# A fifth buffer for gathered expert rows in a mixture-of-experts kernel

## The chip, the cores and the metric

The kernel runs on one core of a Trainium2 chip. A core has TensorE (PE, matmuls; its weight loads are shown apart as PEld), VectorE (DVE), ScalarE (ACT), GpSimd (POOL) and SyncE (SP), each with its own instruction stream, joined by counting semaphores, and 16 DMA engines that carry transfers issued from SP's and POOL's queues. The metric is the device time of one execution in microseconds (us).

## The reference

The input is 4 sequences of 1024 tokens by 512 channels. Two residual blocks are computed: a time-mix attention with a linear recurrence, and a feed-forward block of a shared part and 64 routed experts.

```
x = x + layernorm(attention(layernorm(x)))
h = layernorm(x)
idx, w = router(h)              # 64 experts, 8 groups, best 4 groups, best 6 experts per token
                                # scores = sigmoid(h @ gate_w.T); the choice uses scores + e_bias
shared = relu(h @ su.T)**2 @ sd.T            # 512 -> 1024 -> 512
for each expert e:                           # at most 128 tokens each
    rows   = h[tokens of e]                  # 128 x 512
    y      = relu(rows @ w1[e].T)**2 @ w2[e].T   # 512 -> 256 -> 512
    routed[tokens of e] += gate * y
x = x + layernorm(shared + routed)
```

## The kernel before, in words

The 4096 tokens are worked on as 8 tiles of 512. After the attention and the routing, a long stretch interleaves two jobs in an order written out by hand: the shared part of tiles 3 to 7 (each 8 steps of an up and a down matmul group), and the 64 experts, two to a step from step 2 of tile 3 on (`experts_in`), ending with two steps of tile 7 done; the remaining steps of tile 7 hold no expert. At the end the sums are loaded back, normalised and added to the residual.

The layout of memory: `h` in HBM holds each token's normalised row of 512 and, behind it, its 64 gates (576 numbers in all, 288 KB for 128 tokens). `ysh` holds the shared part's result, to which the experts add.

One expert e goes through these steps:

- **Index.** DVE copies column e of the token list into one of four columns of `gather_token` (`index_gather`, L1643). For e of 4 and above it first waits until PE has turned expert e-4.
- **Gather.** POOL issues an indirect DMA of 128 rows of `h` into `xd_sb[e % 4]` (`gather`, L1196), after the index and after the turning of expert e-4. Three of the four buffers lie in the tile that the profile calls xres, one in xnd.
- **Turn.** PE transposes the rows in four pieces (`xd_transpose`, L668; here it waits for the rows), ACT copies them out (L1021).
- **First layer.** 16 small matmuls with w1 (`e_first`, L679), ACT takes relu and square (L1027, L1029), DVE squares and takes the rest of the rounding (`e_square`, L1657 and L1659).
- **Second layer.** w2 is split by ACT (`w2_round`, L1037) and DVE (`w2_rest`, L1663), then six matmuls (`e_second`, L694 to L696).
- **Gate.** ACT scales the result by the gate into one of four `e_out` buffers (`e_gate`, L1045, tile k_sb).
- **Scatter.** POOL issues an indirect DMA that adds the 128 rows into `ysh` (L1222). It waits for the gate step of e and for the landing of scatter e-1, since two experts may add to the same token.

The order on each engine at expert e matters. PE: turn e+2, first layer e+1, second layer e. ACT: copy of e+2, relu and square of e+1, gate e, split of w2 for e+1. DVE: square of e+1, then `index_scatter(e+1)` (L1650, L1652: the scatter's token column and the gate column, four of each; it waits for the landing of scatter e-3 and for the turning of e+1), then `index_gather(e+5)`, then `w2_rest(e+1)`. POOL: gather e+5, then scatter e. Before expert 0, POOL issues gathers 0 to 3, and at expert 0 gathers 4 and 5 before scatter 0. SP loads w1 and w2 (512 KB each, L369, four buffers each) as PE frees them, and a tile of `ht` (1 MB, L362) per tile of the shared part.

Small constants of the routing lie in the tile mixf as one row of 1024 numbers per partition (`consts`): the bias row in 0 to 63, expert numbers, masks, place numbers, and in 488 to 499 the three groups of four index and gate columns. Most of them have no reader once the token list is made.

Of the kernel before, what the change touches and what calls it, by code (L numbers as in the profile page):

```python
# [8 lines left out]
U32 = mybir.dt.uint32  # L9
# [5 lines left out]
C = 512  # L15
# [3 lines left out]
TT = 512  # L19
# [9 lines left out]
SJ = SH // P  # L29
IK = HID // P  # L30
ROUTE_SCALE = 2.5
EB, WB = 4, 4
LOWEST = 3e38
ROUTED = 3
RS = 3
# [11 lines left out]
def sandwich(nc, t):  # L47

    ctx = ExitStack()
    with ctx:  # L50
# [76 lines left out]
        yout_ready ysh_stored logits_done score_ready sel_ready pos_ready placed route_step gates_ready gates_stored hots_ready tabled table_ready  # L127
        gather_index scatter_index xd_turned xdT_ready e_up e_relu e_hi_ready e_square e_lo_ready w2_hi_ready w2_lo_ready e_down e_gated added
        out_stored o_summed ln4_stats ln4_moments ln4_based ln4_rstd o_joined o_normed o_ready o_added""".split()
        names += [f"{n}{q}" for n, b in (("w1_loaded", WB), ("w2_loaded", WB), ("xd_loaded", EB)) for q in range(b)]  # L130
        names += [f"{n}{k}" for n in ("ysh_loaded", "x1_loaded") for k in range(NT)]
        S = {n: sem(n) for n in names}

# [6 lines left out]
        def flat(tile):  # L140
            return tile[:, :, :].rearrange("p a b -> p (a b)")
# [14 lines left out]
        youts = [v_sb] * (ROUTED + 1) + [hb, sr, xin]  # L156
        consts = flat(mixf)
        bias_row = consts[:, 0:E]
        number = consts[:, E:2 * E]
        causal = consts[:, 128:192].bitcast(BF16)  # L160
        ones = consts[:, 192:256].bitcast(BF16)
# [6 lines left out]
        place_64 = consts[:, 640:640 + CAP]  # L168
        number_1 = consts[:, 768:768 + E]
        blank_row = consts[:, 832:833]  # L170
        gather_token = consts[:, 488:488 + EB].bitcast(U32)
        scatter_token = consts[:, 492:492 + EB].bitcast(U32)
        e_gates = consts[:, 496:496 + EB]
        scratch = flat(xnd)
        at = [0]

# [39 lines left out]
                 [state_flat[:, b * CK * HID:(b + 1) * CK * HID] for b in range(2)]  # L216
        w1_sb = [w.rearrange("p (k i) -> p k i", k=CK) for w in halves[0::2]]
        w2_sb = [w.rearrange("p (k c) -> p k c", k=IK) for w in halves[1::2]]
        xd_sb = [flat(xres)[:, q * (C + E):(q + 1) * (C + E)] for q in range(EB - 1)] + [scratch[:, 0:C + E]]
        xdT = [flat(xnT)[:, q * C:(q + 1) * C].rearrange("p (k n) -> p k n", k=CK) for q in range(EB)]  # L220
        e_hidden = [flat_run_max[:, b * HID:(b + 1) * HID] for b in range(2)]
        e_hi = [e_split[:, (2 + b) * HID:(3 + b) * HID] for b in range(2)]
# [69 lines left out]
        def within(e, ahead):  # L292
            return not (isinstance(e, int) and e + ahead >= E)
# [190 lines left out]
        def _(pe):  # L484
# [175 lines left out]


            def xd_transpose(e):
                q = e % EB
                pe.wait_ge(S[f"xd_loaded{q}"], 16 * (e // EB + 1))
                if e > 0:
                    pe.wait_ge(S["xdT_ready"], e)
                for c in range(CK):
                    mm = pe.transpose(turn_bank[:, c * P:(c + 1) * P], xd_sb[q][:, c * P:(c + 1) * P], ident[:, :])  # L668
                mm.then_inc(S["xd_turned"], 1)
# [449 lines left out]
        def _(pool):  # L1119
# [68 lines left out]
            scale_and_offset(3, NT - 1)  # L1188

            def gather(e):  # L1190
                q = e % EB
                pool.wait_ge(S["gather_index"], e + 1)
                if e >= EB:
                    pool.wait_ge(S["xd_turned"], e - EB + 1)
                pool.sem_inc(S["pool_step"], 1)
                pool.indirect_dma_start(xd_sb[q], None, t["h"], bass.IndirectOffsetOnAxis(ap=gather_token[:, q:q + 1], axis=0)).then_inc(S[f"xd_loaded{q}"], 16)  # L1196

# [2 lines left out]
            pool.wait_ge(S["h_blank"], 16)  # L1200
            pool.wait_ge(S["gates_stored"], 16 * NT)
            pool.wait_ge(S["h_lo_ready"], CK * (ROUTED + 1))
            for e in range(EB):
                gather(e)


# [1 line left out]
            def expert(e):  # L1208
                q = e % EB
                if first(e):  # L1210
                    gather(EB)
                if within(e, EB + 1):
                    gather(e + EB + 1)
                pool.wait_ge(S["e_gated"], e + 1)
                pool.wait_ge(S["scatter_index"], 2 * e + 2)
                if first(e):
                    pool.wait_ge(S["ysh_stored"], 16 * ROUTED)
                    pool.wait_ge(S["ysh_blank"], 16 * (1 + NT - ROUTED))
                else:
                    pool.wait_ge(S["added"], 16 * e)  # L1220
                pool.sem_inc(S["pool_step"], 1)
                pool.indirect_dma_start(t["ysh"], bass.IndirectOffsetOnAxis(ap=scatter_token[:, q:q + 1], axis=0), e_out[q], None,  # L1222
                                        compute_op=ALU.add).then_inc(S["added"], 16)
# [38 lines left out]
        def _(dve):  # L1262
# [373 lines left out]
                dve.tensor_tensor(s_lo[:, j % 3, :], square[:, j % 2, :], s_hi[:, j % 3, :].bitcast(F32), ALU.subtract).then_inc(S["s_lo_ready"], 1)  # L1636

            def index_gather(e):
                q = e % EB
                if e >= EB:  # L1640
                    dve.wait_ge(S["xd_turned"], e - EB + 1)
                    dve.sem_inc(S["dve_step"], 1)
                dve.tensor_copy(gather_token[:, q:q + 1], token_list[:, e:e + 1]).then_inc(S["gather_index"], 1)  # L1643

            def index_scatter(e):
                q = e % EB
                if e >= EB:
                    dve.wait_ge(S["added"], 16 * (e - EB + 1))
                    dve.sem_inc(S["dve_step"], 1)
                dve.tensor_copy(scatter_token[:, q:q + 1], token_list[:, e:e + 1]).then_inc(S["scatter_index"], 1)  # L1650
                dve.wait_ge(S["xd_turned"], e + 1)
                dve.tensor_copy(e_gates[:, q:q + 1], xd_sb[q][:, C + e:C + e + 1]).then_inc(S["scatter_index"], 1)  # L1652

            def e_square(e):
                b = e % 2
# [9 lines left out]
            def expert(e):  # L1665
                if e == 0:
                    index_scatter(0)
                    e_square(0)
                    w2_rest(0)
                if within(e, 1):  # L1670
                    e_square(e + 1)
                    index_scatter(e + 1)
                if e == 0:
                    index_gather(EB)
                if within(e, EB + 1):
                    index_gather(e + EB + 1)
                if within(e, 1):
                    w2_rest(e + 1)

            def tile(k):  # L1680
# [6 lines left out]
                for j in range(SJ):  # L1687
# [4 lines left out]
                    if k < ROUTED:  # L1692
                        if i == 1:
                            counted(r - 1, route_bank)
                        next_rest(*range(CK))
                        if i == 0 and r >= 2:
                            group_experts(r - 1)
                            experts_chosen(r - 1)
                        if i == 1:
                            hots(r - 1)  # L1700
                        if i == 2 and r < NT:
                            groups(r)
                        if n == 2:
                            ln3(NT - 1)
                    else:
                        todo = list(experts_in(k, j))
                        if k == ROUTED and j == 0:
                            list_tokens()
                            for e in range(EB):
                                index_gather(e)  # L1710
                        next_rest(0)
                        for e in todo[:1]:
                            expert(e)
                        next_rest(1)
                        for e in todo[1:2]:
                            expert(e)
                        next_rest(2)
                        for e in todo[2:]:
                            expert(e)
                        next_rest(3)  # L1720
# [74 lines left out]
```

## Time and profile before

| | us |
|---|---|
| median of 3 runs | 1281.77 |
| lowest and highest | 1281.32, 1287.52 |
| the profiled execution, its own time | 1278.08 |
| its span, first to last instruction | 1276.1 |
| busy: PE, DVE, ACT, POOL | 1151.0, 872.0, 682.9, 295.4 |

How to read it: the span is what the profile's positions are counted in, and the execution's time is 2.0 us more. Busy times are sums over an engine's instructions. A DMA's issue on POOL is counted as a POOL instruction; the transfer itself runs on after it, and "landing" is when its last part has arrived. A row names a line of the kernel and the tiles written and read, without buffer numbers.

### The profile page before, as it was taken

Reading aid. Unit: us, or ns where it says so; the run is one execution under the profiler, and the core shown is the slowest. Engines: PE = TensorE matmul, PEld = TensorE weight load, DVE = VectorE, ACT = ScalarE, POOL = GpSimd, SP = SyncE. Lnnn points to the kernel's source line nnn. Section 1 sums busy time; section 2 is a strip of 40 time slices with the busy share of each in tenths; the row PEclk is TensorE's granted clock in tenths of the full one; section 3 lists DMA queues with packets and bytes.
Section 4 is the critical chain, followed back from the end, with each engine's and each line's share of the span. In section 5 each row is a group of like instructions: output and inputs, shape, how many; then the busy total and the mean of one; then the engine's idle time right before and its main releaser. Section 6 shows DMA issues by size and latency. Waiting matters only on the chain.

```text
span 1276.1 us, 15911 instructions
## 1 busy us (share of the span) xinstructions
PE 1151.0 (90%) x5080; PEld 784.8 (61%) x5080; DVE 872.0 (68%) x2093; ACT 682.9 (54%) x1121; POOL 295.4 (23%) x268
## 2 busy tenths in 40 slices
PE   5997999899899997779999889999998999999893
PEld 2443444444344443457888768888887788788761
DVE  4598979897988898759888964444444344444384
ACT  2455656665667566763324235565555456555343
POOL 2010102020202001210000013443343443344255
PEclk9998999999999998789999999999999999999997
DMA  8401022222122241496534238989888888998798
GB/s 307 171 6 34 0 67 69 66 73 82 47 70 68 54 99 69 132 279 222 168 109 137 71 99 230 250 221 289 240 228 253 227 245 221 279 249 201 177 316 339
DMA packets 79520, 206.19 MB, mean 162 GB/s; under 512 B 10192, under 2 KB 10320, under 8 KB 76624
## 3 DMA queue, kind: packets, MB, share of 16 engines
q1 hardware_dynamic: 59408, 156.98, 35.3%
q0 software_dynamic: 20032, 48.24, 20.0%
q8 instruction: 38, 0.62, 0.2%
q14 instruction: 42, 0.34, 0.1%
HBM read 145.93 MB, written 59.28 MB: 161 GB/s over the span
## 4 chain that ended last, share of the span: by engine, by line
PE 26%; DMA 18%; DVE 6%; issue 3%; ACT 2%; POOL 2%; SPq 1%; POOLq 0%; DVEq 0%; ACTq 0%
DMA ysh<-k_sb,mixf 13%; PE bank L679 4%; PE bank L654 2%; PE bank L636 2%; PE bank L655 2%; PE bank L656 2%; PE bank L638 2%; PE bank L637 2%; DMA xnd<-h,mixf 2%; DMA xnd<-ysh 2%; PE bank L498 1%; DMA xres<-h,mixf 1%; PE bank L668 1%; PE bank L694 1%; PE bank L695 1%
## 5 line engine op out<-in xcount | busy, mean ns | idle before, releaser
L541 PE MATMUL bank<-mix_ring,weights 128*128 128x512 f32 x768 | 343.5, 605 | 14.2 <-ACT xres L848 7.0
L541 PEld LDWEIGHTS bank<-mix_ring,weights 128*128 128x128 f32 x768 | 147.2, 194 | 199.6 <-issue 193.2
L1222 POOL DMA_INDIRECT ysh<-k_sb,mixf x64 | 109.0, 1703 | 235.2 <-DVE mixf L1643 79.6
L548 PE MATMUL bank<-weights,rw 128*128 128x512 f32 x256 | 118.5, 618 | 12.5 <-ACT sr L807 9.0
L993 ACT ACTIVATE k_sb<-bank 128x512 f32<-128x512 f32 x64 | 38.2, 597 | 146.3 <-PE bank L638 146.2
L636 PE MATMUL bank<-h_high,ffn_w 128*128 128x512 f32 x256 | 102.9, 402 | 2.7 <-ACT k_sb L993 2.7
L1657 DVE TENSOR_TENSOR run_max<-run_max 128x256 f32<-128x256 f32 x64 | 27.2, 425 | 114.2 <-ACT e_split L1029 114.2
L654 PE MATMUL bank<-ffn_w,s_split 128*128 128x512 f32 x256 | 102.2, 399 | 0.3 <-DVE s_split L1636 0.3
L637 PE MATMUL bank<-h_low,ffn_w 128*128 128x512 f32 x256 | 100.9, 394 | 0.0
L638 PE MATMUL bank<-h_high,ffn_w 128*128 128x512 f32 x256 | 100.8, 394 | 0.0
L655 PE MATMUL bank<-ffn_w,s_split 128*128 128x512 f32 x256 | 100.7, 393 | 0.0
L656 PE MATMUL bank<-ffn_w,s_split 128*128 128x512 f32 x256 | 100.3, 392 | 0.0
L1196 POOL DMA_INDIRECT xres<-h,mixf x48 | 53.0, 1103 | 200.0 <-DVE mixf L1643 182.8
L548 PEld LDWEIGHTS bank<-weights,rw 128*128 128x128 f32 x256 | 50.4, 199 | 78.2 <-issue 66.1
L1133 POOL TENSOR_SCALAR rstd<-mv 128x4 f32<-128x4 f32 x16 | 9.9, 619 | 377.7 <-DVE mv L1285 369.7
L679 PE MATMUL bank<-xnT,wkv 128*128 128x128 f32 x768 | 93.7, 275 | 0.1
L1633 DVE TENSOR_TENSOR k_sb<-k_sb 128x512 f32<-128x512 f32 x64 | 44.1, 689 | 72.6 <-ACT k_sb L993 72.1
L1663 DVE TENSOR_TENSOR wkv_split<-wkv,xnd_split 128x1024 fp32r<-128x1024 f32 x48 | 58.8, 1224 | 47.4 <-ACT xnd_split L1037 45.9
L679 PEld LDWEIGHTS bank<-xnT,wkv 128*128 128x128 f32 x768 | 89.5, 192 | 0.3 <-issue 0.3
L1314 DVE SCALAR_TENSOR_TENSOR mix_ring<-xnd,vecs,xnT 128x512 f32<-128x512 f32 x96 | 70.1, 745 | 4.2 <-PE bank L541 2.1
L1045 ACT ACTIVATE k_sb<-bank,mixf 128x512 f32<-128x512 f32 x64 | 44.1, 689 | 48.1 <-PE bank L696 43.1
L694 PE MATMUL bank<-xnd_split,e_split 128*128 128x512 f32 x128 | 55.9, 436 | 10.5 <-ACT e_split L1029 6.7
(227 smaller groups left out, 2302.1 us busy)
## 6 DMA issues: line engine op xcount, KB each, us to landing
wkv<-in_w SPq DMA_DIRECT2D x96, 512.0 KB
state<-in_w SPq DMA_DIRECT2D x32, 512.0 KB
xin<-in_x SPq DMA_DIRECT2D x8, 1024.0 KB, 5.4
xin<-h SPq DMA_DIRECT2D x8, 1024.0 KB, 6.4
xres<-in_x POOLq DMA_DIRECT2D x7, 1024.0 KB, 9.2
h<-hb SPq DMA_DIRECT2D x7, 1024.0 KB, 4.5
x<-xres SPq DMA_DIRECT2D x7, 1024.0 KB, 6.8
ht<-xnT SPq DMA_DIRECT2D x7, 1024.0 KB, 8.2
```

What stands on the lines that cost most here:

```text
L541: mm = pe.matmul(bank[:, d, :], W(j)[:, ck, d * P:(d + 1) * P], mix_slot(4 * j + ck), start=(ck == 0), stop=(ck == CK - 1))
L548: mm = pe.matmul(bank[:, s, :], rw[:, ck, s * P:(s + 1) * P], W(3)[:, ck, :], start=(ck == 0), stop=(ck == CK - 1))
L636: pe.matmul(up_bank, hi, hT_hi[:, ck, :], start=(ck == 0), stop=False)
L637: pe.matmul(up_bank, hi, hT_lo[:, ck, :], start=False, stop=False)
L638: mm = pe.matmul(up_bank, lo, hT_hi[:, ck, :], start=False, stop=(ck == CK - 1))
L654: pe.matmul(y_bank[:, s, :], hi, w_hi, start=(j == 0), stop=False)
L655: pe.matmul(y_bank[:, s, :], hi, w_lo, start=False, stop=False)
L656: mm = pe.matmul(y_bank[:, s, :], lo, w_hi, start=False, stop=(j == SJ - 1 and k < NT - 1))
L679: mm = pe.matmul(e_up_bank[:, i * CAP:(i + 1) * CAP], w1_sb[e % WB][:, ck, i * P:(i + 1) * P], xdT[q][:, ck, :], start=(ck == 0), stop=(ck ...
L694: pe.matmul(route_bank, act_hi[:, i, :], hi[:, i, :], start=(i == 0), stop=False)
L1222: pool.indirect_dma_start(t["ysh"], bass.IndirectOffsetOnAxis(ap=scatter_token[:, q:q + 1], axis=0), e_out[q], None, compute_op=ALU.add).t ...
L1314: dve.scalar_tensor_tensor(out=mix_slot(n), in0=xnd[:, ck, :], scalar=vecs[:, MK + j, ck:ck + 1], in1=xnT[:, ck, 0:TT], op0=ALU.mult, op1= ...
```

## The change

The gather gets five buffers (`XB = 5`) in place of four; everything counted by `EB` (scatter columns, gate columns, `e_out`, `xdT`) stays at four. The fifth buffer is numbers 448 to 1023 of the constants' row, where the routing's place numbers and masks lay. The index and gate columns, which lay inside that stretch, move into the bias row (numbers 0 to 4, 16 to 19 and 32 to 35). POOL issues gathers 0 to 4 ahead, gathers 5 and 6 at expert 0, and gather e+6 before scatter e. DVE writes the index column of e+6 where it wrote that of e+5. A gather waits for the turning of the expert five before it, so gather e+6 waits for that of e+1, as gather e+5 did.

```diff
--- before.py
+++ after.py
@@ -29,7 +29,7 @@
 SJ = SH // P
 IK = HID // P
 ROUTE_SCALE = 2.5
-EB, WB = 4, 4
+EB, WB, XB = 4, 4, 5
 LOWEST = 3e38
 ROUTED = 3
 RS = 3
@@ -127,7 +127,7 @@
         yout_ready ysh_stored logits_done score_ready sel_ready pos_ready placed route_step gates_ready gates_stored hots_ready tabled table_ready
         gather_index scatter_index xd_turned xdT_ready e_up e_relu e_hi_ready e_square e_lo_ready w2_hi_ready w2_lo_ready e_down e_gated added
         out_stored o_summed ln4_stats ln4_moments ln4_based ln4_rstd o_joined o_normed o_ready o_added""".split()
-        names += [f"{n}{q}" for n, b in (("w1_loaded", WB), ("w2_loaded", WB), ("xd_loaded", EB)) for q in range(b)]
+        names += [f"{n}{q}" for n, b in (("w1_loaded", WB), ("w2_loaded", WB), ("xd_loaded", XB)) for q in range(b)]
         names += [f"{n}{k}" for n in ("ysh_loaded", "x1_loaded") for k in range(NT)]
         S = {n: sem(n) for n in names}
 
@@ -156,6 +156,8 @@
         youts = [v_sb] * (ROUTED + 1) + [hb, sr, xin]
         consts = flat(mixf)
         bias_row = consts[:, 0:E]
+        gather_token, scatter_token, e_gates = (consts[:, n * E // 4:n * E // 4 + w] for n, w in enumerate((XB, EB, EB)))
+        gather_token, scatter_token = gather_token.bitcast(U32), scatter_token.bitcast(U32)
         number = consts[:, E:2 * E]
         causal = consts[:, 128:192].bitcast(BF16)
         ones = consts[:, 192:256].bitcast(BF16)
@@ -168,9 +170,6 @@
         place_64 = consts[:, 640:640 + CAP]
         number_1 = consts[:, 768:768 + E]
         blank_row = consts[:, 832:833]
-        gather_token = consts[:, 488:488 + EB].bitcast(U32)
-        scatter_token = consts[:, 492:492 + EB].bitcast(U32)
-        e_gates = consts[:, 496:496 + EB]
         scratch = flat(xnd)
         at = [0]
 
@@ -216,7 +215,7 @@
                  [state_flat[:, b * CK * HID:(b + 1) * CK * HID] for b in range(2)]
         w1_sb = [w.rearrange("p (k i) -> p k i", k=CK) for w in halves[0::2]]
         w2_sb = [w.rearrange("p (k c) -> p k c", k=IK) for w in halves[1::2]]
-        xd_sb = [flat(xres)[:, q * (C + E):(q + 1) * (C + E)] for q in range(EB - 1)] + [scratch[:, 0:C + E]]
+        xd_sb = [flat(xres)[:, q * (C + E):(q + 1) * (C + E)] for q in range(3)] + [scratch[:, 0:C + E], consts[:, 2 * TT - C - E:2 * TT]]
         xdT = [flat(xnT)[:, q * C:(q + 1) * C].rearrange("p (k n) -> p k n", k=CK) for q in range(EB)]
         e_hidden = [flat_run_max[:, b * HID:(b + 1) * HID] for b in range(2)]
         e_hi = [e_split[:, (2 + b) * HID:(3 + b) * HID] for b in range(2)]
@@ -660,8 +659,8 @@
 
 
             def xd_transpose(e):
-                q = e % EB
-                pe.wait_ge(S[f"xd_loaded{q}"], 16 * (e // EB + 1))
+                q = e % XB
+                pe.wait_ge(S[f"xd_loaded{q}"], 16 * (e // XB + 1))
                 if e > 0:
                     pe.wait_ge(S["xdT_ready"], e)
                 for c in range(CK):
@@ -1188,10 +1187,10 @@
             scale_and_offset(3, NT - 1)
 
             def gather(e):
-                q = e % EB
+                q = e % XB
                 pool.wait_ge(S["gather_index"], e + 1)
-                if e >= EB:
-                    pool.wait_ge(S["xd_turned"], e - EB + 1)
+                if e >= XB:
+                    pool.wait_ge(S["xd_turned"], e - XB + 1)
                 pool.sem_inc(S["pool_step"], 1)
                 pool.indirect_dma_start(xd_sb[q], None, t["h"], bass.IndirectOffsetOnAxis(ap=gather_token[:, q:q + 1], axis=0)).then_inc(S[f"xd_loaded{q}"], 16)
 
@@ -1200,7 +1199,7 @@
             pool.wait_ge(S["h_blank"], 16)
             pool.wait_ge(S["gates_stored"], 16 * NT)
             pool.wait_ge(S["h_lo_ready"], CK * (ROUTED + 1))
-            for e in range(EB):
+            for e in range(XB):
                 gather(e)
 
 
@@ -1208,9 +1207,9 @@
             def expert(e):
                 q = e % EB
                 if first(e):
-                    gather(EB)
-                if within(e, EB + 1):
-                    gather(e + EB + 1)
+                    gather(XB)
+                if within(e, XB + 1):
+                    gather(e + XB + 1)
                 pool.wait_ge(S["e_gated"], e + 1)
                 pool.wait_ge(S["scatter_index"], 2 * e + 2)
                 if first(e):
@@ -1636,9 +1635,9 @@
                 dve.tensor_tensor(s_lo[:, j % 3, :], square[:, j % 2, :], s_hi[:, j % 3, :].bitcast(F32), ALU.subtract).then_inc(S["s_lo_ready"], 1)
 
             def index_gather(e):
-                q = e % EB
-                if e >= EB:
-                    dve.wait_ge(S["xd_turned"], e - EB + 1)
+                q = e % XB
+                if e >= XB:
+                    dve.wait_ge(S["xd_turned"], e - XB + 1)
                     dve.sem_inc(S["dve_step"], 1)
                 dve.tensor_copy(gather_token[:, q:q + 1], token_list[:, e:e + 1]).then_inc(S["gather_index"], 1)
 
@@ -1649,7 +1648,7 @@
                     dve.sem_inc(S["dve_step"], 1)
                 dve.tensor_copy(scatter_token[:, q:q + 1], token_list[:, e:e + 1]).then_inc(S["scatter_index"], 1)
                 dve.wait_ge(S["xd_turned"], e + 1)
-                dve.tensor_copy(e_gates[:, q:q + 1], xd_sb[q][:, C + e:C + e + 1]).then_inc(S["scatter_index"], 1)
+                dve.tensor_copy(e_gates[:, q:q + 1], xd_sb[e % XB][:, C + e:C + e + 1]).then_inc(S["scatter_index"], 1)
 
             def e_square(e):
                 b = e % 2
@@ -1671,9 +1670,9 @@
                     e_square(e + 1)
                     index_scatter(e + 1)
                 if e == 0:
-                    index_gather(EB)
-                if within(e, EB + 1):
-                    index_gather(e + EB + 1)
+                    index_gather(XB)
+                if within(e, XB + 1):
+                    index_gather(e + XB + 1)
                 if within(e, 1):
                     w2_rest(e + 1)
 
@@ -1706,7 +1705,7 @@
                         todo = list(experts_in(k, j))
                         if k == ROUTED and j == 0:
                             list_tokens()
-                            for e in range(EB):
+                            for e in range(XB):
                                 index_gather(e)
                         next_rest(0)
                         for e in todo[:1]:
```

## Rows read from the trace of the kernel before

**Rows 1.** The profile's page, shares of the chain that ended last, by engine and line.

```profile
PE 26%; DMA 18%; DVE 6%; issue 3%; ACT 2%; POOL 2%; SPq 1%; POOLq 0%; DVEq 0%; ACTq 0%
```

**Rows 2.** The scatter's line: duration ns min/median/max, first and last start; then landing.

```profile
L1222 POOL DMA_INDIRECT ysh<-k_sb,mixf x64: 1552/1588/2614, 776.1 to 1205.7; - x64
...
DMA to landing us min/median/max: 4.8/5.6/10.4
```

**Rows 3.** Chain of waits, 944 to 981 us: start, us, what.

```profile
944.15 5.75 DMA ysh<-k_sb,mixf
...
950.80 5.68 DMA ysh<-k_sb,mixf
...
963.21 7.67 DMA ysh<-k_sb,mixf
...
971.77 8.81 DMA ysh<-k_sb,mixf
```

**Rows 4.** The gate step's line, 770 to 916.3 us.

```profile
L1045 ACT ACTIVATE k_sb<-bank,mixf x23: 687/689/692, 772.1 to 916.2; 128x512 f32<-128x512 f32 x23
```

**Rows 5.** The scatter's line, 770 to 916.3 us.

```profile
L1222 POOL DMA_INDIRECT ysh<-k_sb,mixf x20: 1568/1588/2496, 776.1 to 910.6; - x20
```

**Rows 6.** ACT in order of time (start, us, engine, line): the last gate step.

```profile
1196.14 0.69 ACT L1045 ACTIVATE k_sb<-bank,mixf 128x512 f32<-128x512 f32 x1 [3.58 <-PE bank L696]
```

**Rows 7.** Chain of waits, 1200 us to the end.

```profile
1205.74 4.76 DMA ysh<-k_sb,mixf
...
1211.48 19.57 DMA xnd<-ysh
```

**Rows 8.** DVE in order of time, 1231 us; in brackets the idle time and its end.

```profile
1231.07 1.29 DVE L1738 BATCH_NORM_STATS2 stats<-xnd 128x6 f32<-128x512 f32 x2 [0.44 <-DMA xnd<-ysh]
```

**Rows 9.** Waits of PE, 770 to 1200 us: us in total, times, longest.

```profile
PE bank L668 <- DMA xnd<-h,mixf: 6.3, 5, 1.5
PE bank L668 <- DMA xres<-h,mixf: 4.9, 5, 1.6
```

**Rows 10.** POOL in order of time, at expert 0, in the middle, at the end.

```profile
772.60 0.95 POOL L1196 DMA_INDIRECT xres<-h,mixf  x1 [7.84 <-DVE mixf L1643]
773.86 1.96 POOL L1196 DMA_INDIRECT xres<-h,mixf  x1 [0.30 <-issue]
776.12 1.65 POOL L1222 DMA_INDIRECT ysh<-k_sb,mixf  x1 [0.30 <-issue]
...
924.99 2.17 POOL L1222 DMA_INDIRECT ysh<-k_sb,mixf  x1 [4.99 <-DVE mixf L1643]
927.46 0.99 POOL L1196 DMA_INDIRECT xnd<-h,mixf  x1 [0.30 <-issue]
...
1171.91 1.46 POOL L1196 DMA_INDIRECT xnd<-h,mixf  x1 [0.30 <-issue]
```

**Rows 11.** Waits of DVE, 770 to 1200 us.

```profile
DVE mixf L1650 <- DMA ysh<-k_sb,mixf: 17.4, 15, 3.9
```

**Rows 12.** Chain of waits, the scatter at 917 us.

```profile
916.92 7.17 DMA ysh<-k_sb,mixf
```

**Rows 13.** DVE in order of time, 924 us.

```profile
924.23 0.15 DVE L1650 CAST mixf<-xnd 128x1 uint32<-128x1 f32 x1 [1.27 <-DMA ysh<-k_sb,mixf]
...
924.48 1.21 DVE L1663 TENSOR_TENSOR wkv_split<-wkv,xnd_split 128x1024 fp32r<-128x1024 f32 x1
```

**Rows 14.** PE in order of time, 927 us.

```profile
927.31 0.48 PE L694 MATMUL bank<-xnd_split,e_split 128*128 128x512 f32 x1
```

**Rows 15.** Stretch 850 to 960: busy of PE, PEld, DVE, ACT, POOL, clock, DMA, GB/s.

```profile
850.00:960.00 110.00, 105.06 (x630) 90.95 (x628) 51.42 (x118) 63.18 (x107) 46.12 (x32) 1.00 0.87 239
```

**Rows 16.** The scatter's landings alone, 1070 to 1186 us.

```profile
DMA to landing us min/median/max: 4.8/5.5/8.1
```

**Rows 17.** Waits of SP's queue, 770 to 1200 us.

```profile
SPq L369 <- PE bank L679: 276.7, 58, 10.1
```

**Rows 18.** SP in order of time, one load.

```profile
973.23 0.38 SPq L362 DMA_DIRECT2D xin<-ht  x1
```

## The prediction

> **What bounds the kernel now.** I read the page first, then the scatter's and gather's lines, the chain of waits, the waits by engine, and last the timelines of POOL, DVE and PE around single experts.
>
> The page's chain gives PE 26% and the DMAs 18% [rows 1], which looks like a PE with holes in it. The holes in question are there: in the experts' stretch PE waits before a turn for gathered rows ten times, 6.3 + 4.9 = 11.2 us in all, at most 1.6 us at once [rows 9]. The change aims at them, so the first question is whether they matter.
>
> The scatters say no. There are 64, the first issued at 776.1, the last at 1205.7 and landed at 1205.74 + 4.76 = 1210.50 [rows 2, 7]. Each waits for the landing of the one before. In the chain, one issued at 944.15 lands 5.75 later, at 949.90, and the next goes out at 950.80 [rows 3]: 0.90 us from landing to issue. So an expert costs the scatter chain its landing plus 0.90. With the median of 5.6 [rows 2] that is 64 x 5.6 + 63 x 0.90 = 415 us of the 1210.5 - 776.1 = 434.4 that the chain lasts; the other 19 us are the long landings (7.67 and 8.81 in [rows 3], 10.4 at most) and little else, since the mean landing that the whole asks for is (434.4 - 56.7)/64 = 5.9. The chain runs back to back from expert 0 to 63.
>
> A second proof is the backlog. By 916.3 us 23 gate steps had begun and 20 scatters [rows 4, 5]: three results of the four that `e_out` can hold lie waiting while the scatter before them is in flight. And the last gate step is at 1196.14 + 0.69 = 1196.83, while the last scatter goes out at 1205.74 [rows 6, 7]. PE is ahead by 8.9 us even at the end. Where the page's chain steps from a scatter through a gather and PE to the next scatter, it follows the gate step that ended last, which belongs to a later expert; by count the scatter at 916.92 is the 21st, and its result was gated two gate steps before the one at 916.2.
>
> The end hangs on that chain too. The sums are loaded once the last scatter has landed: issued 1211.48, 19.57 us [rows 7]. DVE's moments at 1231.07 wait for just that load, by 0.44 us [rows 8], and from there on moments, normalising and adding follow each other to 1276.1. So the end is the scatter chain's end + 65.6 us.
>
> **The change part by part.** The sum is made against the profiled execution (1278.08, span 1276.1, so 2.0 around it); the median of the runs is 3.7 above it, and I add that last.
>
> *Gathers ahead of expert 0.* POOL issues one more. The nearest prices are those of the next two, 0.95 + 0.30 and 1.96 + 0.30: 1.3 to 2.3 us. It falls into the 7.84 us in which POOL waits for DVE's next index, until 772.60 [rows 10]. Gathers 5 and 6 then take the places of 4 and 5 at 772.60 and 773.86, because the waits for turnings come out with the same counts, and scatter 0 stays at 776.12. Cost 0; 2.3 at most if that cover were gone. DVE writes one more index column, 0.15 [rows 13], after the first four, and PE's first turn needs only the first gather. Cost 0.
>
> *Each gather one expert sooner.* In the steady part POOL issues the scatter, then the next gather 0.30 us after it, at 927.46 behind a scatter at 924.99 [rows 10], and then waits for a landing. After the change the same slot holds a gather for the next expert along. The order on POOL's queue, its bytes and its moment relative to the scatters are unchanged, so the scatter chain sees 0. At the far end the last gather (1171.91 [rows 10]) goes out one scatter earlier; one landing there may lose a neighbour. The last landing, without a gather beside it, is 4.76 against a median of 5.6 [rows 2, 7], so the gain is 0 to 0.8, and I take 0.3.
>
> *What PE does with the missing wait.* The rows are there when it asks, so the 11.2 us go from this line. But PE can't pull away, because DVE is tied to the scatters as well: `index_scatter` waits for the landing four before, 15 times visibly, 17.4 us [rows 11]. For example a scatter issued at 916.92 lands at 924.09 [rows 12]; DVE writes the columns at 924.23 and only then w2's rest, 924.48 to 925.69 [rows 13]; PE starts that second layer at 927.31 [rows 14]. PE has 1.6 us to gain there, once and not per expert, until it stands at this wait. The change leaves these columns and `e_out` at four. So I take a PE lead of 1.5 us (0 and 1.6 are the bounds), worth 0 at the end, because neither the scatters nor the load at 1211.48 wait for it. The bubble moves: PE's waits before L694 for `w2_rest` or the squares, and DVE's at L1650, grow by about what L668 loses.
>
> *Columns moved, buffer in another tile.* The copies and the DMAs keep their shapes. The trace has gathers into two tiles, 0.95 us of issue into xres at 772.60 and 0.99 into xnd at 927.46, and 1.96 at most [rows 10]; a third should lie there. From 0.04 less to 1.0 more per gather are the bounds; behind a scatter whose landing POOL waits for, both cost 0, and I take 0.
>
> *What can't be read.* All of this leaves the landing as it is. Its median is 5.6 over all and 5.5 in the last long stretch [rows 2, 16]; 0.1 us less or more on each of the 64 is 6.4 us, and this is my bound on both sides for what a shift of the traffic may do.
>
> Sum: 0 + 0 - 0.3 + 0 = -0.3; 1278.08 - 0.3 = 1277.8 for an execution like the profiled one, and 3.7 more, 1281.5, for the median.
>
> **The rivals.** *Faster: the holes in PE count.* Then the 11.2 us of [rows 9] come off, 1281.8 - 11.2 = 1270.6. PE is 105.06 of 110 us busy from 850 to 960 [rows 15], the fullest engine, which speaks for it. Against it is the backlog of three and more, and that the chain could only end 11 us sooner if each landing were 0.18 us shorter. The Trainium skill (Perfetto Trace Analysis, Identifying Performance Opportunities) speaks for this rival: the engine with the highest occupancy is the one to improve, and the same gap repeated on it can mean too few buffers. The gap is repeated here [rows 9], but the rule doesn't ask whether something slower stands behind that engine; by the rule the time would be this rival's.
>
> *Slower: the traffic shifts onto the scatters.* SP issues the weight loads as PE frees the buffers (276.7 us of its waiting is for L679 [rows 17]). A PE 1.5 us further ahead moves all of these against the scatters, and the DMA engines are 0.87 busy [rows 15]. A scatter that meets a burst is dear: 8.81 at 971.77, with the 1 MB load of the next tile issued at 973.23 [rows 3, 18], 3.2 above the median. If one more is caught at each of four such places (three tile loads and the residual loads behind the last experts) that is 12.8, 1294.6; from three on (9.6) it decides against the 6.4 that count as a change. Against it: bytes and counts are the same, and a burst meets some scatter already. The Trainium skill (DMA: Bandwidth & Descriptors, Queues, rings and completion order) says that an engine's semaphore write lands only after every earlier write of that engine, whatever queue it came from. The trace agrees in so far as [rows 3] has its longest landing beside that load [rows 18], and by this rule the time would be this rival's.
>
> *The gathers aren't sooner.* An index that DVE writes late would hold them where they are; the one at 772.60 waits so [rows 10]. Elsewhere it goes out 0.30 behind its scatter [rows 10], so this touches only the first experts. Time as before, 1281.8.
>
> **How the numbers follow.** Forecast 0.65, holes count 0.17, traffic 0.14, not sooner 0.04. About 0.5% (6.4 us) is what a measurement of this kernel can tell from no change; the runs before spread from 1278.1 to 1287.5. Forecast and not-sooner lie inside: same 0.69; faster 0.17; slower 0.14. The forecast's own range is 1281.5 +- 6.4. I take 1272 to 1290: downwards most of the way to the faster rival's 1270.6; upwards the forecast's edge with the bare lead-in, 1281.5 + 6.4 + 2.3 = 1290.2, which holds two more bursts (6.4) as well. About 0.2 is left out.
>
> **What would show it.** L668's waits for gathered rows under 2 us in place of 11.2; gaps from landing to next scatter still 0.90 and the scatters from about 776 to 1210; more wait at L1650 and before L694; PE's last gate step 0 to 2 us nearer the front; the load of the sums still the start of the tail. I am wrong if the last scatter lands more than 6 us from 1210.5, or if the end moves while it doesn't.

## The result, and the profile after

The changed kernel takes 1295.84 us (median of 4 runs, 1293.29 to 1300.28) where the kernel before took 1281.55 in the same runs: ratio 1.0106, interval 1.0072 to 1.0140. On a second occasion, beside other experiments, the ratio was 1.0047 (1.0018 to 1.0076). It is slower, by 0.5 to 1.1%; the forecast was no change. The kernel before is measured again on each occasion, which is why its time differs from place to place below. A ratio is given with its 95% interval; it is not the quotient of the two medians beside it and can differ from that by up to 0.3%.

The profiled execution took 1293.29 (before 1278.08), its span 1290.5. First the chain of waits at its end (start, us, what), to lay beside [rows 7]:

```profile
1200.03 7.65 DMA ysh<-k_sb,mixf
...
1220.18 4.85 DMA ysh<-k_sb,mixf
...
1226.01 19.46 DMA xnd<-ysh
```

The last scatter lands at 1225.03, 14.5 us later than the 1210.50 before, and the load of the sums follows it as it did. From that landing to the end of the span are 65.5 us, before 65.6. So the whole loss lies ahead of that landing.

The scatter's line, for [rows 2], and POOL in order of time at expert 0, for [rows 10]:

```profile
L1221 POOL DMA_INDIRECT ysh<-k_sb,mixf x64: 1552/2106/2532, 775.7 to 1220.2; - x64
...
DMA to landing us min/median/max: 4.8/5.6/10.3
```
```profile
772.17 0.94 POOL L1195 DMA_INDIRECT xres<-h,mixf  x1 [6.53 <-DVE mixf L1642]
773.42 1.95 POOL L1195 DMA_INDIRECT xres<-h,mixf  x1 [0.30 <-issue]
775.68 1.65 POOL L1221 DMA_INDIRECT ysh<-k_sb,mixf  x1 [0.30 <-issue]
```

The first scatter goes out 0.4 us sooner. The extra gather ahead of it fell into the idle time (6.53 left of 7.84). Median and shortest landing are those of before. The median hides the loss: adding up issue to landing for each of the 64 gives 376.0 us before and 390.9 after, and the 63 gaps from a landing to the next issue give 58.4 and 58.5. Landings over 6.5 us went from 10 to 16.

The waits of PE and of DVE, 770 to 1215 us (us in total, times, longest), for [rows 9, 11]:

```profile
PE bank L693 <- DVE wkv_split L1662: 13.3, 6, 3.7
PE bank L693 <- ACT e_split L1028: 6.7, 7, 1.0
PE bank L693 <- DVE state_split L1662: 6.0, 3, 3.2
```
```profile
DVE mixf L1649 <- DMA ysh<-k_sb,mixf: 95.4, 36, 8.0
```

PE's waits for gathered rows, 11.2 us before, are gone. In their place stand waits for w2's rest (13.3 + 6.0, before 0.6 + 3.2), and DVE waits 95.4 us for the landing four scatters back, before 17.4. DVE comes up to that wait 36 times among the 60 scatters at which there is one, before 15 times. PE is further ahead: the last gate step ends 13.9 us before the last scatter's issue, in the kernel before 8.9; the mean over the 64 is 14.3 us, before 11.6.

A hint of what makes a landing long is seen where a long one lies. In the chain of waits of the changed kernel, and under it SP's queue in order of time around the long one:

```profile
929.38 6.25 DMA ysh<-k_sb,mixf
936.52 8.85 DMA ysh<-k_sb,mixf
946.28 5.42 DMA ysh<-k_sb,mixf
```
```profile
936.95 0.33 SPq L368 DMA_DIRECT2D wkv<-in_w  x1
...
939.14 0.33 SPq L368 DMA_DIRECT2D wkv<-in_w  x1
```

The scatter of 936.52 takes 8.85 us; a 512 KB weight load was sent 0.43 us after it, another 2.62 after. Before, the scatter of 944.15 [rows 3] took 5.75, and its loads had been sent 2.1 and 0.7 us ahead of it:

```profile
942.09 0.33 SPq L369 DMA_DIRECT2D state<-in_w  x1
943.46 0.33 SPq L369 DMA_DIRECT2D wkv<-in_w  x1
```

This became the theory to test (A): a scatter lands late when SP sends weight loads between about 0.6 us before and 2.2 us after its issue, and with a PE no longer held by the gathers more of them go out there. I counted, in each trace, how many weight loads go out in that stretch around each scatter of experts 1 to 56, leaving out the three to five that lie within 6 us of a 1 MB load of ht. "42 x 5.57" stands for 42 scatters whose landings took 5.57 us in the mean:

| kernel | no load | one | two or more | sum of 64 landings | ratio to before |
|---|---|---|---|---|---|
| before | 42 x 5.57 | 10 x 6.35 | 1 x 7.97 | 376.0 | 1 |
| after | 32 x 5.61 | 15 x 6.44 | 4 x 7.21 | 390.9 | 1.0106 |
| after, second time | 29 x 5.56 | 22 x 6.45 | 2 x 7.29 | 391.0 | 1.0047 |
| columns only | 42 x 5.53 | 8 x 5.75 | 3 x 7.50 | 369.9 | 0.9996 |
| PE held | 40 x 5.55 | 11 x 6.59 | 2 x 7.77 | 380.4 | 0.9993 |
| five buffers, old order | 39 x 5.57 | 10 x 6.28 | 4 x 7.38 | 379.6 | 0.9993 |
| first hold, after | 11 x 5.42 | 0 | 42 x 7.37 | 442.8 | 1.0488 |
| first hold, before | 3 x 6.24 | 1 x 4.74 | 49 x 7.19 | 449.7 | 1.0513 |
| later hold, after | 50 x 5.71 | 0 | 1 x 8.33 | 377.7 | 1.0022 |
| later hold, before | 48 x 5.63 | 2 x 6.28 | 1 x 6.71 | 371.4 | 0.9925 |
| later hold, quarters (none left out) | 53 x 5.66 | 2 x 7.51 | 1 x 7.07 | 367.2 | 0.9914 |

For the first hold the profile gives no landing scatter by scatter; there it is the last landing event ahead of the next scatter's issue. The stretch was drawn from the first two traces; the others are tests of it. The columns-only kernel fits it least: one load made 5.75 of 5.53. Counts and sums are those of one profiled execution, ratios those of all runs; the profiled execution of the later hold in the changed kernel took 1284.61, its median is 1289.20. In every kernel of the table the end comes 65.3 to 66.5 us after the last landing.

### The profile page after: what moved, and what is told of

Its sections match the earlier page's. It is cut to its first block, busy times and chain, and to the rows that moved or that the text cites. A ratio compares the mean times of both kernels' runs of the same rounds, so it can differ in the third digit from the quotient of the medians.

```text
span 1290.5 us, 15910 instructions
## 1 busy us (share of the span) xinstructions
PE 1159.5 (90%) x5080; PEld 792.0 (61%) x5080; DVE 871.6 (68%) x2093; ACT 682.5 (53%) x1121; POOL 302.7 (23%) x268
## 4 chain that ended last, share of the span: by engine, by line
DMA 25%; PE 20%; DVE 6%; issue 4%; ACT 1%; SPq 1%; POOL 1%; POOLq 0%; DVEq 0%; ACTq 0%
DMA ysh<-k_sb,mixf 22%; PE bank L678 3%; PE bank L653 2%; PE bank L654 2%; PE bank L655 2%; PE bank L635 2%; PE bank L637 2%; PE bank L636 2%; DMA xnd<-ysh 2%; PE bank L497 1%; DMA xin<-h 1%; DVE stats L1737 1%; PE bank L693 1%; DVE hb L1519 1%; PE bank L694 1%
## 5 line engine op out<-in xcount | busy, mean ns | idle before, releaser
L540 PE MATMUL bank<-mix_ring,weights 128*128 128x512 f32 x768 | 343.6, 605 | 14.0 <-ACT xres L847 6.9
L1221 POOL DMA_INDIRECT ysh<-k_sb,mixf x64 | 123.1, 1923 | 244.1 <-DVE mixf L1642 131.3
L653 PE MATMUL bank<-ffn_w,s_split 128*128 128x512 f32 x256 | 104.3, 408 | 2.0 <-DVE s_split L1635 2.0
L654 PE MATMUL bank<-ffn_w,s_split 128*128 128x512 f32 x256 | 102.5, 400 | 0.0
L655 PE MATMUL bank<-ffn_w,s_split 128*128 128x512 f32 x256 | 102.2, 399 | 0.0
L1195 POOL DMA_INDIRECT xres<-h,mixf x39 | 41.2, 1056 | 192.1 <-DVE mixf L1642 181.1
L693 PE MATMUL bank<-xnd_split,e_split 128*128 128x512 f32 x128 | 56.9, 444 | 26.0 <-DVE wkv_split L1662 13.3
L1649 DVE CAST mixf<-xnd 128x1 uint32<-128x1 f32 x64 | 9.7, 151 | 95.5 <-DMA ysh<-k_sb,mixf 95.4
```

The costliest lines, as they stand in the source:

```text
L540: mm = pe.matmul(bank[:, d, :], W(j)[:, ck, d * P:(d + 1) * P], mix_slot(4 * j + ck), start=(ck == 0), stop=(ck == CK - 1))
L653: pe.matmul(y_bank[:, s, :], hi, w_hi, start=(j == 0), stop=False)
L654: pe.matmul(y_bank[:, s, :], hi, w_lo, start=False, stop=False)
L655: mm = pe.matmul(y_bank[:, s, :], lo, w_hi, start=False, stop=(j == SJ - 1 and k < NT - 1))
L693: pe.matmul(route_bank, act_hi[:, i, :], hi[:, i, :], start=(i == 0), stop=False)
```

## The experiments

**Columns only (cols_only).** Four buffers, old order, the columns in the bias row.

```diff
+gather_token, scatter_token, e_gates = (consts[:, n * E // 4:n * E // 4 + EB] for n in range(3))
-gather_token = consts[:, 488:488 + EB].bitcast(U32)
...
```

> Only the index and gate columns move into the bias row; four buffers and the old order stay. Theory A (the scatters' landings got longer because PE, no longer held by the gathers, sends SP's weight loads at other moments of the scatters' flights): nothing that moves the loads is changed, so within 0.5% of before, about 1281. Theory B (the place of the columns, read by POOL for its descriptors, costs time): a good part of the 14 us shows here, 1288 to 1296, with the scatter's issue longer than 1.6 us.

1281.32 against 1285.58, ratio 0.9996 (0.9956 to 1.0037). The columns' place costs nothing.

**PE held (pe_held).** All of the change, and from expert 4 on PE waits for one gather more.

```diff
 pe.wait_ge(S[f"xd_loaded{q}"], 16 * (e // XB + 1))
+if e >= XB - 1 and e + 1 < E:
+    pe.wait_ge(S[f"xd_loaded{(e + 1) % XB}"], 16 * ((e + 1) // XB + 1))
```

> The changed kernel in full (fifth buffer, gathers one expert sooner, columns moved), but from expert 4 on PE also waits, before it turns expert e, for the landing of gather e+1, which lies in the slot of POOL's queue where gather e lay before. So PE gets its old pace back, and nothing else is undone. Theory A: near before, 1278 to 1287, the sum of the 64 landings near 376 us, at most one landing more over 6.5 us than the 10 of before. Theory B (place of columns or buffer, or gathers in flight earlier): stays near 1295, sum of landings near 391.

1283.10 against 1285.58, ratio 0.9993 (0.9962 to 1.0025). The waits of PE in this kernel, 770 to 1210 us:

```profile
PE bank L669 <- issue: 11.9, 9, 2.0
```

The waits at the turn are back, nine of them with 11.9 us in all (the profile names no releaser for them), and the loss is gone, with the fifth buffer, its place and all the earlier gathers left in. The sum of landings is 380, near before; landings over 6.5 us are 14, which is more than I had allowed, so in this one trace the count says less than the time.

**Cut w1 loads (w1_small_before, w1_small_after).**

```diff
+part = slice(0, CK * HID if e < WB or name == "w2" else 64)
-sp.dma_start(dst[e % WB]..., t[name][e])
+sp.dma_start(dst[e % WB]...[:, part], t[name][e][:, part])
```

> The kernel before with the w1 loads of experts 4 to 63 cut to 32 KB of 512 KB each (the buffers keep the w1 of experts 0 to 3 for the most part, so what is computed is not the reference's); semaphores, order and instructions stay. Theory A: the scatters meet half the traffic; median landing near the 4.8 us of the last experts to 5.2, sum of landings 376 down to 310-340, time 1235 to 1260. If landings don't depend on the loads: 1281.

> The changed kernel with the same cut of the w1 loads. Theory A: the loads no longer bunch, so the 14 us between the two kernels shrink to under 5; the time is within 5 us of the cut kernel before. Theory B (columns, buffer, or the issue of the descriptors beside DVE's split of w2): the 14 us stay, as none of that is cut.

1266.05 and 1267.68 against 1285.58: ratios 0.9857 (0.9794 to 0.9920) and 0.9869 (0.9806 to 0.9933). With about half the weight bytes the two kernels are 1.6 us apart, within their intervals. The landings fell to sums of 343.6 and 341.6, as expected, but the time fell less than I had written: in these kernels PE sets the end. The last gate step and the scatter's line of the changed kernel with the cut:

```profile
1184.93 0.69 ACT L1045 ACTIVATE k_sb<-bank,mixf 128x512 f32<-128x512 f32 x1 [4.45 <-PE bank L696]
```
```profile
L1222 POOL DMA_INDIRECT ysh<-k_sb,mixf x64: 1552/1589/1806, 777.8 to 1188.4; - x64
...
DMA to landing us min/median/max: 4.6/5.1/8.5
```

The last scatter goes out 2.8 us behind the last result, the gaps from a landing to the next issue hold 15 to 17 us more than 0.90 each, and from the last landing to the end are 71.4 and 72.4 us, where the other kernels have about 65.6. So these two runs say that the loss goes when the traffic falls and the chain stops setting the end; they don't say by which of the two.

**Five buffers, old order (five_old_order).** Gathers go four ahead and e+5 at expert e, as before.

```diff
-for e in range(XB):
+for e in range(EB):
...
-    gather(e + XB + 1)
+    gather(e + EB + 1)     # index_gather likewise
```

> Five buffers and the columns in the bias row, but gathers issued in the old order (four ahead, then e+5 before scatter e); only the wait for a turned buffer is loosened, which was never the last one. Theory A: PE's waits for rows come back and with them the old pace, 1278 to 1287. A rival by which the use of the constants' tile for rows costs time: between 1285 and 1295.

1285.79 against 1288.58, ratio 0.9993 (0.9962 to 1.0023). The time lies in both of the ranges written above; the ratio to the kernel before of the same occasion decides. PE's waits in it, 770 to 1210 us, show the rows asked for again, from the constants' tile too:

```profile
PE bank L667 <- DMA xres<-h,mixf: 8.6, 7, 2.3
...
PE bank L667 <- DMA mixf<-h,mixf: 2.0, 1, 2.0
```

So of the change's three parts only the earlier gather costs time, and by the run with PE held it does so only where it lets PE go ahead.

**Two chains (two_chains).** Kernel before, odd experts' scatters into a second tensor that nobody reads; half of the routed sum is left out.

```diff
-pool.wait_ge(S["added"], 16 * e)
+pool.wait_ge(S[f"added{e % 2}"], 16 * (e // 2))
-pool.indirect_dma_start(t["ysh"], ...)
+pool.indirect_dma_start(t[("ysh", "ysh2")[e % 2]], ...)
```

> The kernel before with the scatters of odd experts sent to a second tensor that nobody reads (so half of the routed sum is left out); each scatter waits only for the one two before. If the chain of scatters is what sets the end, it ends where PE sets it: last landing before 1205 in place of 1210.5 and the time at the floor of the kernels with cut loads, 1262 to 1270. If PE or the loads set the end, 1281.

1266.72 against 1288.58, ratio 0.9839 (0.9806 to 0.9873). ACT's last gate step and the scatter's line:

```profile
1183.91 0.69 ACT L1046 ACTIVATE k_sb<-bank,mixf 128x512 f32<-128x512 f32 x1 [4.36 <-PE bank L697]
```
```profile
L1223 POOL DMA_INDIRECT ysh<-k_sb,mixf x64: 1552/1675/1695, 777.1 to 1185.4; - x64
```

The scatters follow the gate steps by 2.0 us in most places, where a gather's issue stands between, and by 0.8 at the end. The single chain of scatters is what held the kernel before, and about 1266 us is what PE needs without it. The changed kernel wasn't run so; its gaps, 58.5 us against 58.4, show the same chain.

**The first hold (locked_after, locked_before).** SP waits for a count that POOL's queue raises when it passes a gather.

```diff
 # SP, expert e
+sp.wait_ge(S["gathered"], min(E, e + (6 if e < 12 else 5) + 1))   # kernel before: 5 and 4
 # POOL, behind the gather
+pool.sem_inc(S["gathered"], 1)
```

> The changed kernel, and SP sends the weight loads of expert e only once POOL has issued a given gather (e+6 for e under 12, then e+5), so that they can't go out in the first 2.5 us of a scatter's flight. Theory A (phase of loads against scatters): scatters with no weight load issued from 0.6 us before to 2.2 us after them land in 5.5 to 5.6 us in both kernels, those with one in 6.5 to 7.0, those with two in 7.2 or more; with nearly all in the first class the sum of the landings falls from 391 to 350-370, the time to 1266-1276, no worse than before. Rival C (more bytes in flight or a PE further ahead cost by themselves, whatever the phase): stays near 1295, or worse, as loads are only delayed.

> The same hold of SP's loads in the kernel before (gather e+5 for e under 12, then e+4, which lie in the same slots of POOL's queue). Theory A: it has 15 scatters with a load beside them too, so it gains less than the changed kernel: 1268 to 1278. If both locked kernels come out alike, the fifth buffer is worth nothing once the phase is fixed. Rival C: 1281 or slower.

1350.97 and 1352.62 against 1288.58: ratios 1.0488 (1.0453 to 1.0523) and 1.0513 (1.0481 to 1.0545), far above what A gave, and on the side of rival C ("or worse", "or slower"). I had meant the loads to go out behind the gather. Of the changed kernel under this hold: the scatter's landing in the chain of waits, POOL, and SP, each in order of time.

```profile
927.03 6.85 DMA ysh<-k_sb,mixf
...
934.78 6.90 DMA ysh<-k_sb,mixf
```
```profile
927.03 2.17 POOL L1223 DMA_INDIRECT ysh<-k_sb,mixf  x1 [5.56 <-DVE mixf L1644]
929.51 0.99 POOL L1196 DMA_INDIRECT xres<-h,mixf  x1 [0.30 <-issue]
934.78 2.17 POOL L1223 DMA_INDIRECT ysh<-k_sb,mixf  x1 [4.28 <-DVE mixf L1644]
```
```profile
935.20 0.33 SPq L368 DMA_DIRECT2D wkv<-in_w  x1
935.58 0.42 SPq L368 DMA_DIRECT2D state<-in_w  x1
```

The scatter goes out at 934.78 and the two loads at 935.20 and 935.58, before the gather behind that scatter has begun. From 870 to 1240 us 43 of these loads wait for the count, so POOL's queue raises it while the scatter is still being issued. From expert 14 to 56 both loads go out 0.4 and 0.8 us after nearly every scatter. That is the bad moment, held for 42 and 49 counted scatters, and they land in 7.37 and 7.19 us. Experts 1 to 11 of the changed kernel, whose loads went out about 4 us into the flight, land in 5.42. By accident this is the strongest test of what A says of a load's moment. It left rival C standing, that the hold itself costs.

**The later hold (late_after, late_before).** The same wait; the count now comes from an instruction on POOL itself. In the changed kernel both holds also raise another counter in place of `pool_step`, for which nothing waits.

```diff
-pool.sem_inc(S["gathered"], 1)
+if e > 0:
+    pool.wait_ge(S["gathered"], e)
+pool.memset(consts[:, E - 4:E - 3], 0.0).then_inc(S["gathered"], 1)
```

> The changed kernel, with SP's weight loads of expert e held until a one-column memset on POOL that stands behind the gather (gather e+6 for e under 12, then e+5), so that they go out some 4 us into a scatter's flight, not at 0.4 and 0.8 us as in the first hold. Theory A (the moment of the loads within a scatter's flight sets its landing): scatters with their loads there land in 5.4 us, as experts 1 to 11 did under the first hold; sum of landings 345 to 365, time 1266 to 1276, thus 70 us less than the first hold for 3.5 us of shift. Rival C (holding the loads costs by itself, by full buffers or a starved PE): again 1300 or more.

> The same later hold in the kernel before (gather e+5, then e+4). Theory A: 1266 to 1278, and within 5 us of the changed kernel under the same hold. Rival C: 1300 or more.

1289.20 and 1278.98 against 1286.37: ratios 1.0022 (0.9996 to 1.0048) and 0.9925 (0.9899 to 0.9952). POOL and SP of the kernel before with this hold:

```profile
924.14 1.59 POOL L1226 DMA_INDIRECT ysh<-k_sb,mixf  x1 [4.10 <-DMA ysh<-k_sb,mixf]
926.03 0.99 POOL L1197 DMA_INDIRECT xnd<-h,mixf  x1 [0.30 <-issue]
927.02 0.11 POOL L1200 MEMSET mixf<- 128x1 f32 x1
```
```profile
927.16 0.33 SPq L369 DMA_DIRECT2D wkv<-in_w  x1
927.54 0.42 SPq L369 DMA_DIRECT2D state<-in_w  x1
```

The same loads, held by the same kind of wait, 3.0 and 3.4 us into the flight in place of 0.4 and 0.8: 62 us faster in the changed kernel and 74 in the one before (the two holds ran on different occasions, on which the kernel before differed by 2 us). Rival C falls. But A had 1266 to 1276 for the changed kernel, and it took 1289.20, which isn't faster than before and is 5 us under the changed kernel without a hold (1294.05 on the same occasion); the kernel before with the hold gained 0.75% where more was written. Landings without a load are 5.63 (before) and 5.71 (changed), not 5.4. And the changed kernel stays 10 us behind the other under the same hold, where I had written at most 5. With hardly a load left in the stretch (3 counted scatters before, 1 in the changed kernel), the two kernels are as far apart as without a hold. That is against A as the whole cause of the loss.

**The changed kernel again (after_again).**

> The changed kernel once more beside the others on this chip. Theory A: 1288 to 1300, with more scatters over 6.5 us than before has, though not the same ones, since their places come from the drift of the loads against the scatters and not from single instructions.

1294.05 against 1286.37, ratio 1.0047 (1.0018 to 1.0076). 24 counted scatters have a load beside them, where the first trace of this kernel has 19 and the kernel before 11; 18 landings are over 6.5 us. The loss is there a second time, and smaller.

**Quarters (late_quarters).** The later hold in the kernel before, and each ht load in four parts.

```diff
-if e in rounded_before:
-    load_shared_h(rounded_before[e])
+for c in range(CK):
+    if e - c in rounded_before:
+        load_quarter(rounded_before[e - c], c)        # 256 KB
```

> The kernel before with the later hold, and the 1 MB loads of the next tile's ht (three of them among the experts) sent as four loads of 256 KB, one behind the weight loads of each of four experts. Theory A: the four or five scatters that now land in 7 to 9.8 us beside such a load come down to about 6; with 371 us of landings before, 360 to 366 after, and a time 4 to 10 us under the 1279 of the later hold alone: 1269 to 1275. If those landings have another cause (the end of a tile on PE and ACT), 1277 to 1281.

1275.08 against 1284.68, ratio 0.9914 (0.9887 to 0.9941). From 874 to 1186 us the scatter's line reads:

```profile
DMA to landing us min/median/max: 4.8/5.6/6.8
```

At the second and third of the three tile loads the landings of 8.6 and 9.8 us are gone. The first lies ahead of that stretch: there the scatter of 865.39 still takes 8.2 us, 8.8 with the whole load. What all of it gave back (371.4 to 367.2) is 4 us; the time, 1275.08, is at the upper edge of what was written, and the ratio can't be told from that of the later hold alone. It is faster than the kernel before by 0.9%.

## Why the prediction was wrong

*What bounds the kernel* held. The chain of scatters runs back to back (gaps 58.4 and 58.5), the end is its last landing + 65.6 (65.5 after), and with the chain cut in two the time falls to where PE sets it. The sign that the prediction gave for being wrong came: the last landing is 14.5 us from 1210.5, and the end moved with it. PE's 11.2 us of waits were worth nothing, as forecast; their removal was worth less than nothing.

*Gathers ahead of expert 0* and *columns moved* held: first scatter at 775.68 for 776.12; ratio 0.9996 for the columns.

*Each gather one expert sooner* held as far as POOL goes. The 0.3 us at the end can't be seen among the rest.

*What PE does with the missing wait* is the step that failed: "a PE lead of 1.5 us [...], worth 0 at the end, because neither the scatters nor the load at 1211.48 wait for it". Of the first half the kind is right and the size is not: where the rows are ready PE does come up to DVE's wait (17.4 us of it before, 95.4 after), and the bubble moved as said, but the lead at the end grew by 5.0 us and in the mean by 2.8, outside the bounds of 0 and 1.6. The second half, the price of 0, is wrong: putting PE's wait back alone, with all else of the change left in, removes the loss (ratio 0.9993). The scatters don't wait for PE, but SP's loads do, and the moment of the loads can set how long a scatter flies (62 and 74 us between the two holds). That the loss of the change itself came by this way is read from the table, not shown by a run. Of the 14.9 us more of landings, counted against 5.55 us each: 10.7 come from the scatters in the table (11.2 us of excess before, 21.9 after), 1.9 from those beside ht loads, 4.2 from the last seven, two of which land in 6.55 and 7.65, and 1.9 less from expert 0.

*What can't be read* gave 6.4 us as bound on the landings. They moved by 14.9. The bound came from the medians of two stretches, and medians don't see a change in how many landings are long; the mean of 5.9 beside a median of 5.6, which the prediction had in hand, was the sign.

The rival *traffic shifts* had it, at a chance of 0.14: loads that follow PE move against the scatters, price 12.8, time 1294.6. Its place was right in part. It was set on three tile loads and the residual loads behind the last experts, and there lie 1.9 + 4.2 us of the 14.9 (the 7.65 at 1200.03 is one of the last); the larger part, 10.7, lies beside the ordinary weight loads, all along. So that 1294.6 comes so near to the measured 1295.84 is in part luck; by the second occasion's ratio it would be 1287.8. By the rule of the Trainium skill given there (DMA: Bandwidth & Descriptors, Queues, rings and completion order), an engine's semaphore write lands only after its earlier writes on every queue. The runs agree in so far that a load delays a landing, but loads sent 2.1 and 0.7 us before a scatter left it at 5.75, and those sent 0.43 and 2.62 after made it 8.85, which the rule as it stands doesn't tell apart.

What stays open is why this stretch is the bad one, and how much of the loss is A's. Under the later hold the changed kernel is still 10 us behind. In the two profiled executions its landings sum to 377.7 against 371.4; 3.5 of these 6.3 us lie in the last seven scatters, and its gaps are 3.1 us longer, mostly by one of 4.4 us ahead of expert 12, where the hold's count changes.

A rival that no run here separates is the scatter's own issue: with DVE's split of w2 beside it, it takes over 2 us in place of 1.59. The number of such issues goes with the loss in every pair:

| pair | issues over 2 us | time |
|---|---|---|
| before; after, and a second time | 11; 36, 36 | after slower by 0.5 to 1.1% |
| columns only, PE held, five buffers in the old order | 8, 11, 10 | as before |
| later hold: before, after | 2, 26 | after slower by 10 us |
| first hold: before, after | 42, 43 | alike |
| cut w1 loads: before, after | 2, 0 | alike |

Within one trace the evidence is mixed. Among landings without a load beside them, those with a long issue and those with a short one are 5.62 and 5.56 in the kernel before, 5.59 and 5.65 in the changed one, but 5.79 and 5.48 with PE held, 5.87 and 5.48 with five buffers in the old order, and 5.96 and 5.51 with the later hold in the changed kernel. Long issues come where DVE has just waited for a landing [rows 13], so they may be no more than a sign that PE is ahead. Nor is the size of the loss settled beyond 0.5 to 1.1%.

## What to carry to other kernels

When a serial chain of transfers sets the time, look at what every freed engine sends onto the same DMA engines, and when. A wait that costs nothing where it stands may keep an engine at a pace that suits the chain, as PE's waits did here. Compare sums or means of landings, since here a dozen longer ones among 64 leave the median where it was; and once the moment is known, tie the loads to the chain with an instruction that runs there, not with one that a queue passes ahead of time.

## What the runs showed of the hardware

- The moment at which loads go out, with the same bytes and counts, is worth 62 us in the changed kernel (1350.97 with both loads mostly 0.4 and 0.8 us behind each scatter, 1289.20 at 3 to 5 us) and 74 us in the kernel before (1352.62 and 1278.98).
- A semaphore raised by POOL's queue behind a gather was seen by SP 0.4 us after the scatter ahead of that gather began; raised by a memset behind the gather, 3.0 us after.
- A scatter's issue on POOL took 1.59 us or, with DVE's 1.2 us split of w2 beginning 0.5 us ahead of it, 2.16. Before 11 of 64 took over 2 us, after 36. Whether such an issue also lengthens the landing differs from trace to trace: by nothing in the changed kernel (5.59 against 5.65), by 0.45 us with the later hold in it (5.96 against 5.51).
